# Selective scan with a feed-forward block: VectorE adds the last operand of each half's sums, and TensorE's x projection, a group sum and dt change places with the output projection

## The chip, the cores and the metric

The kernel runs on one core of a Trainium2 chip. The metric is the time on the device of one execution, in microseconds (us), as the median of several runs. Five engines run their own instruction streams in order and meet at semaphores: TensorE (PE, with its weight loads as PEld), VectorE (DVE), ScalarE (ACT), GpSimd (POOL) and SyncE (SP), which issues nearly all DMAs.

## The reference, cut to what matters

Everything is fp32: 4096 rows of 1024. A state-space block with 2048 channels and 16 states per channel is followed by a feed-forward block with dequantised weights.

```python
proj = layernorm(x) @ in_proj_w                    # x and z, 2048 channels each
xc = silu(conv4(x) + conv_b)                       # 4 taps along the rows
dt_r, B, C = rmsnorm of (xc @ x_proj_w.T)          # 64 + 16 + 16
dt = softplus(dt_r @ dt_proj_w + dt_bias)
h_t = exp(dt_t * A) * h_{t-1} + dt_t * B_t * xc_t  # per channel, 16 states
y_t = sum over the 16 states of h_t * C_t
y = (y + D * xc) * silu(z)
x = x + y @ out_proj_w
x = x + layernorm(x) @ W + bias                    # feed-forward
```

The sum over the 16 states and the gating `(y + D * xc) * silu(z)` are what the change touches.

## The kernel before, in words

The 4096 rows are cut into 16 chunks (`c`) of 256 rows (T = 256), the 2048 channels into 8 pairs (`j`) of two 128-channel tiles. One step is one pair of one chunk; steps are numbered S = 8c + j, 128 in all. The chunks overlap as a pipeline: while step (c, j) runs the scan of chunk c, TensorE also does the x input projection and x_proj for chunk c + 1, the output projection for chunk c - 1 and the feed-forward block for chunk c - 2. Steps 1 to 5 of a chunk are alike (plain steps, below). Step 6 has in addition the first layer norm's statistics on VectorE (`norm1_stats`); step 7 the transposes of those rows, the rms norm and the second norm's statistics (`norm2_stats`); step 0 the transposes of the second norm. Chunk 1 has no feed-forward part yet, chunk 0 no output projection either, and chunk 15 no x part any more.

The scan of one pair is 16 units (`unit`, `scan`, `product`, u = 0 to 15), each of two states of one tile, in one of four PSUM banks `hb`. For unit u, ScalarE writes exp(dt*A) into `hb` (L1061), GpSimd makes dt*x*B for four states at a time into `dbx` (L486), VectorE scans in place (L1342) and multiplies by C into `hc` (L1290). Two units make a group of four states; there are eight groups k of a step, four for each tile (half a of the pair, k = 4a + q). For every group:

- GpSimd adds one half of `hc` to the other into `half[:, k % 4]`, 128x512 (`group_sum` of GpSimd, L494), which leaves two operands of 256 columns;
- TensorE adds both operands to the bank `ys[a]` with the identity as weights (`group_sum` of TensorE, L574, two matmuls of 256 columns). ScalarE has put D*x there before (L1080).

After the fourth group of a half VectorE multiplies `ys[a]` by the gate into `ybuf` (`y_gate`, L1301). Below, the gate of half 0 of step S is called y0; it stands behind the product of unit 9. The gate of half 1, y1 (`late_y`), is done in the next step, behind the product of unit 1.

All orders are written out by hand in the bodies of `step`. TensorE's in a plain step (each name a piece of work): ffn (L689), groups 6 and 7 of the step before, out_proj 0, x_proj (L604), out_proj 1 (all out_proj: L767), group 0, x_in_proj 0 (L594), group 1, x_in_proj 1, group 2, out_proj 2, group 3, dt_proj (L624), out_proj 3, z_in_proj 1 (L614), group 4, z_in_proj 0, group 5. In steps 7 and 0 the transposes (L581) stand between, with x_proj behind the first four.

Waits that matter here: x_proj writes into `ys[1]` and waits for y1; z_in_proj 1 writes into `ys[0]` and waits for y0; dt_proj writes into `ys[1]` too and waits until VectorE has taken x_proj's result (`pair_ss`, L1253); VectorE's `add_ffn` (L1272), which stands behind the product of unit 0, waits for ffn; `add_out` (L1272) waits for out_proj 3; ScalarE's softplus (L991, L992) waits for dt_proj, and GpSimd's dtx (L512, L516) for the softplus. ScalarE's `silus` (L1070, L951) stand behind unit 3 and give `xcn`, for which the transposes of steps 7 and 0 and x_proj wait.

## Time and profile before

| | us |
|---|---|
| median of 3 runs (lowest, highest) | 4699.61 (4698.31, 4702.74) |
| the profiled execution | 4697.21 |
| its span | 4695.4 |
| TensorE busy, matmuls | 4448.9 (95%) |
| VectorE busy | 4160.0 (89%) |
| GpSimd busy | 4039.2 (86%) |
| ScalarE busy | 3542.4 (75%) |

The mean granted clock of TensorE is 0.972 of full speed. On the chain of work that ended last TensorE has 59% and VectorE 20%. Matmuls are pipelined: in the timeline the busy time of a group of matmuls includes a tail of about 0.17 us that lies beside the next one; the chain shows them without it. VectorE's instructions overlap their neighbours by 0.08 to 0.09 us in the same way, so what one takes in the stream is read from the start of one to the start of the next.

### The profile page before, as it was taken

The numbers are of one execution on the slowest core, as the hardware profiler recorded it, in microseconds if no ns is written. First come the engines' busy times: TensorE is split into PE (matmuls) and PEld (weight loads), VectorE is DVE, ScalarE is ACT, GpSimd is POOL, SyncE is SP. The second block draws the span as 40 slices with busy tenths as digits, with TensorE's granted clock in tenths as the row PEclk, the third lists the DMA queues.
The fourth block names the chain that finished last, engine by engine and source line by source line (L and its number), as shares of the span: only waits on it lengthen the run. The fifth ranks groups of instructions, "written<-read, shape, count | busy, mean of one in ns | idle before, by whom it ended". The sixth has DMA issues, their size and how long they took to land.

```text
span 4695.4 us, 80181 instructions
## 1 busy us (share of the span) xinstructions
PE 4448.9 (95%) x26656; PEld 4049.0 (86%) x26656; DVE 4160.0 (89%) x5745; ACT 3542.4 (75%) x8848; POOL 4039.2 (86%) x2942
## 2 busy tenths in 40 slices
PE   7788989999999999999999999999999999999889
PEld 6567879989898998989989898998989889898779
DVE  3898989989899998989989899998989989899981
ACT  3777787877778787777877878787787777778760
POOL 0898989989898998989989898998989899899990
PEclk9889999999999999999999999999999999999999
DMA  7324243353434435343353534334353443434232
GB/s 255 130 79 161 99 159 139 114 186 133 173 129 161 145 138 175 124 178 128 123 188 123 177 137 165 137 128 173 138 180 120 145 165 129 165 127 155 90 115 94
DMA packets 160285, 678.56 MB, mean 145 GB/s; under 512 B 21120, under 2 KB 30080, under 8 KB 110720
## 3 DMA queue, kind: packets, MB, share of 16 engines
q1 hardware_dynamic: 141440, 639.88, 39.0%
q10 hardware_dynamic: 18432, 33.56, 1.9%
q8 instruction: 212, 3.47, 0.3%
q14 instruction: 201, 1.65, 0.1%
HBM read 618.32 MB, written 55.05 MB: 143 GB/s over the span
## 4 chain that ended last, share of the span: by engine, by line
PE 59%; DVE 20%; POOL 7%; issue 6%; ACT 5%; DMA 1%; SPq 0%; DVEq 0%; POOLq 0%; ACTq 0%
PE g L767 13%; PE gx L594 13%; PE ys L574 12%; DVE hb L1342 11%; PE ys L614 9%; PE g L689 4%; POOL dbx L486 4%; DVE hc L1290 4%; DVE gx L1238 2%; POOL half L494 2%; PE ys L604 2%; DVE bst L1218 2%; PE gx L581 2%; ACT hb L1061 1%; PE hb L853 1%
## 5 line engine op out<-in xcount | busy, mean ns | idle before, releaser
L1342 DVE TENSOR_TENSOR_SCAN hb<-hb,dbx 128x512 f32<-128x512 f32 x2048 | 2498.0, 1220 | 108.0 <-ACT hb L1061 84.4
L486 POOL TENSOR_TENSOR dbx<-dtx,bb 128x1024 f32<-128x1024 f32 x1024 | 2421.0, 2364 | 60.1 <-DVE hb L1342 34.9
L1061 ACT ACTIVATE hb<-dt,a_neg 128x256 f32<-128x256 f32 x4096 | 1789.5, 468 | 66.3
L494 POOL TENSOR_TENSOR half<-hc 128x512 f32<-128x512 f32 x1024 | 1303.1, 1273 | 135.4 <-DVE hc L1290 120.4
L1290 DVE TENSOR_TENSOR hc<-hb,cb 128x512 f32<-128x512 f32 x2048 | 1378.9, 673 | 0.0
L574 PE MATMUL ys<-half,ident 128*128 128x256 f32 x4096 | 1073.2, 389 | 133.4 <-POOL half L494 119.2
L574 PEld LDWEIGHTS ys<-half,ident 128*128 128x128 f32 x4096 | 757.2, 194 | 254.3 <-POOL half L494 151.3
L767 PEld LDWEIGHTS g<-wo,ybuf 128*128 128x128 f32 x7680 | 954.0, 198 | 20.2 <-issue 1.3
L767 PE MATMUL g<-wo,ybuf 128*128 128x128 f32 x7680 | 966.7, 281 | 0.6 <-issue 0.6
L614 PE MATMUL ys<-xnT,wz 128*128 128x256 f32 x4096 | 928.8, 380 | 1.6 <-DVE ybuf L1301 1.6
L594 PE MATMUL gx<-xnT,wx 128*128 128x256 f32 x3968 | 904.5, 381 | 4.3 <-DMA wx<-in_win 2.6
L1057 ACT COPY hstate<-hb 128x2 f32<-128x2 f32 x2044 | 319.3, 156 | 757.7 <-DVE hc L1290 754.5
L614 PEld LDWEIGHTS ys<-xnT,wz 128*128 128x128 f32 x4096 | 770.6, 191 | 103.1 <-DVE ybuf L1301 2.8
L594 PEld LDWEIGHTS gx<-xnT,wx 128*128 128x128 f32 x3968 | 756.9, 192 | 108.5 <-DMA wx<-in_win 3.0
L689 PEld LDWEIGHTS g<-wf,x2nT 128*128 128x128 f32 x3552 | 414.1, 192 | 5.7
L689 PE MATMUL g<-wf,x2nT 128*128 128x128 f32 x3552 | 414.5, 275 | 0.0
L1301 DVE TENSOR_TENSOR ybuf<-ys,gate 128x256 f32<-128x256 f32 x256 | 107.0, 418 | 237.8 <-PE ys L574 237.6
L1238 DVE SCALAR_TENSOR_TENSOR gx<-xpre,convw,gx 128x256 f32<-128x256 f32 x744 | 302.0, 482 | 13.8 <-ACT gx L942 13.8
L512 POOL TENSOR_TENSOR dtx<-dt,xcs 128x2 f32<-128x2 f32 x128 | 25.3, 198 | 282.7 <-ACT dt L992 176.8
L604 PE MATMUL ys<-xprojw,xcn 128*128 128x96 f32 x1024 | 152.0, 298 | 26.6 <-ACT xcn L951 23.5
L604 PEld LDWEIGHTS ys<-xprojw,xcn 128*128 128x128 f32 x1024 | 143.2, 215 | 33.9 <-issue 21.5
L1067 ACT ACT_TABLE_LOAD x128 | 164.2, 1283 | 2.3
(105 smaller groups left out, 2766.1 us busy)
## 6 DMA issues: line engine op xcount, KB each, us to landing
wz<-in_win SPq DMA_DIRECT2D x128, 1024.0 KB, 4.8
wx<-in_win SPq DMA_DIRECT2D x124, 1024.0 KB, 4.8
wo<-in_wout SPq DMA_DIRECT2D x123, 1024.0 KB, 4.9
wf<-wf_scratch SPq DMA_DIRECT2D x113, 512.0 KB, 3.2
xc_scratch<-xcn ACTq DMA_DIRECT2D x128, 256.0 KB, 2.1
xcs<-xc_scratch SPq DMA_DIRECT2D x128, 256.0 KB, 5.0
bb<-bc_scratch SPq DMA_DIRECT2D x64, 512.0 KB, 7.5
cb<-bc_scratch SPq DMA_DIRECT2D x64, 512.0 KB, 6.7
```

What stands on the lines that cost most here:

```text
L486: nc.gpsimd.tensor_tensor(dbx[:, k % 2, :].rearrange("p (n t) -> p n t", n=NQ), dtx[:, S % 2, a, :].unsqueeze(1).to_broadcast([P, NQ, T]), ...
L494: nc.gpsimd.tensor_tensor(half[:, k % 4, :], hc[:, k % 2, 0:HALF], hc[:, k % 2, HALF:GW], ALU.add).then_inc(halves, 1)
L574: mm = nc.tensor.matmul(ys[a][:, 0:T], ident[:], half[:, k % 4, i * T:(i + 1) * T], start=False, stop=(q == NQ - 1 and i == 1), skip_group ...
L594: mm = nc.tensor.matmul(pair_bank(q)[:, a * T:(a + 1) * T], pair_weights(q)[:, kk, a * P:(a + 1) * P], xnT[:, chunk % 2, kk, :], start=(kk ...
L604: mm = nc.tensor.matmul(ys[1][:, tt * E:(tt + 1) * E], xcn[:, a * T + tt * P:a * T + (tt + 1) * P], xprojw[:, 2 * (q % PAIRS) + a, :], sta ...
L614: mm = nc.tensor.matmul(ys[0][:, a * T:(a + 1) * T], wz[:, kk, a * P:(a + 1) * P], xnT[:, q // PAIRS % 2, kk, :], start=(kk == 0), stop=(k ...
L689: mm = nc.tensor.matmul(g1[:, tt * P:(tt + 1) * P], x2nT[:, kk, tt * P:(tt + 1) * P], wf[:, kk, :], start=(kk == 0), stop=(kk == KH - 1))
L767: mm = nc.tensor.matmul(g1[:, tt * P:(tt + 1) * P], ybuf[:, (1 - st.parity) * PAIRS + kt // 2, (kt % 2) * T + tt * P:(kt % 2) * T + (tt + ...
L1061: ins = nc.scalar.activation(h[:, m * T:(m + 1) * T], dt[:, j % 2, a, :], ACT.Exp, scale=a_neg[:, ds((2 * j + a) * N + 2 * v + m, 1)])
L1238: nc.vector.scalar_tensor_tensor(bank[:, a * T:(a + 1) * T], xpre[:, a, tap:tap + T], convw[:, ds((2 * jq + a) * KC + tap, 1)], bank[:, a ...
L1290: nc.vector.tensor_tensor(hc[:, k % 2, w * UW:(w + 1) * UW], hb[u % 4][:], cb[:, n:n + 2, :].rearrange("p n t -> p (n t)"), ALU.mult).then ...
L1342: nc.vector.tensor_tensor_scan(h[:], h[:], dbx[:, k % 2, w * UW:(w + 1) * UW], 0.0, ALU.mult, ALU.add).then_inc(scans, 1)
```

## The change

VectorE takes over one operand of the last group of each half (k = 3 and k = 7): TensorE does one matmul there in place of two, and a new function `last_sum` adds the other operand, `half[:, 3, T:2T]`, to `ys[a]` in PSUM. It waits for TensorE's matmul of the group. The gate y0 or y1 comes one scan later than before: `last_sum`, scan, gate, where there was gate, scan. GpSimd's sums for k = 3 and k = 7 now also wait until the gate before has been made. On TensorE, x_proj of steps 1 to 6 (and of the others without transposes) stands behind out_proj 1 in place of ahead of it, and group 3 and dt_proj stand ahead of out_proj 2 in place of behind it.

```diff
             def group_sum(S, k):
                 pool.wait_ge(hcs, after(UNITS * S + 2 * k + 2))
                 pool.wait_ge(sum_mm, after(8 * S + k - 3))
+                if k % NQ == NQ - 1:
+                    pool.wait_ge(y_ready, after(2 * S + k // NQ))
...
                 pe.wait_ge(halves, after(8 * SG + k + 1))
-                for i in range(2):
+                for i in range(1 if q == NQ - 1 else 2):
                     mm = nc.tensor.matmul(ys[a][:, 0:T], ident[:], half[:, k % 4, i * T:(i + 1) * T],
-                                          start=False, stop=(q == NQ - 1 and i == 1), skip_group_check=True)
+                                          start=False, stop=(q == NQ - 1), skip_group_check=True)
...
                     else:
                         out_proj(0)
-                        x_proj()
                     out_proj(1)
                     if not (first and st.ffn or last and st.norm1):
+                        x_proj()
                         group(0)
...
                     group(2)
-                    out_proj(2)
                     group(3)
                     dt_proj()
+                    out_proj(2)
                     out_proj(3)
...
+            def last_sum(SP, a):
+                k = NQ * (a + 1) - 1
+                dve.wait_ge(sum_mm, after(8 * SP + k + 1))
+                dve.wait_ge(halves, after(8 * SP + k + 1))
+                nc.vector.tensor_tensor(ys[a][:, 0:T], ys[a][:, 0:T], half[:, k % 4, T:HALF], ALU.add
+                                        ).then_inc(summed, 1)
+
             def y_gate(SP, a):
...
-                dve.wait_ge(sum_mm, after(8 * SP + NQ * (a + 1)))
+                dve.wait_ge(summed, after(2 * SP + a + 1))
...
                     product(1)
+                    late_sum()
+                    scan(3)
                     late_y()
-                    scan(3)
                     product(2)
...
                     product(9)
+                    last_sum(S, 0)
+                    scan(11)
                     y_gate(S, 0)
-                    scan(11)
                     product(10)
```

`late_sum` is `last_sum` of the step before for half 1. The end of the program has one `last_sum` ahead of its last gate.

TensorE in a plain step before, from groups 6 and 7 of the step before to dt_proj (`ys<-half` the group sums, `g<-wo` out_proj, `ys<-xprojw` x_proj, `gx<-xnT` x_in_proj, `ys<-ssmT` dt_proj):

```order
L574 MATMUL ys<-half,ident 128x256 x4
L767 MATMUL g<-wo,ybuf 128x128 x8
L604 MATMUL ys<-xprojw,xcn 128x96 x4
L767 MATMUL g<-wo,ybuf 128x128 x8
L574 MATMUL ys<-half,ident 128x256 x2
L594 MATMUL gx<-xnT,wx 128x256 x8
L574 MATMUL ys<-half,ident 128x256 x2
L594 MATMUL gx<-xnT,wx 128x256 x8
L574 MATMUL ys<-half,ident 128x256 x2
L767 MATMUL g<-wo,ybuf 128x128 x8
L574 MATMUL ys<-half,ident 128x256 x2
L624 MATMUL ys<-ssmT,dtw 128x256 x2
```

The same place with the change:

```order
L579 MATMUL ys<-half,ident 128x256 x3
L772 MATMUL g<-wo,ybuf 128x128 x16
L609 MATMUL ys<-xprojw,xcn 128x96 x4
L579 MATMUL ys<-half,ident 128x256 x2
L599 MATMUL gx<-xnT,wx 128x256 x8
L579 MATMUL ys<-half,ident 128x256 x2
L599 MATMUL gx<-xnT,wx 128x256 x8
L579 MATMUL ys<-half,ident 128x256 x3
L629 MATMUL ys<-ssmT,dtw 128x256 x2
L772 MATMUL g<-wo,ybuf 128x128 x16
```

Groups 6 and 7 have three matmuls in place of four, and so have groups 2 and 3, which now stand together. x_proj (`ys<-xprojw`) has moved behind the 16 matmuls of out_proj 0 and 1, and the third part of out_proj behind dt_proj, next to the fourth.

VectorE around the gate y1 before (`hb` the scans, `hc` the products):

```order
L1272 TENSOR_TENSOR x<-g,x 128x2x128 [waits f_mm,bias_add]
L1342 SCALAR_TENSOR_TENSOR hb<-hb,dbx 128x512 [waits exps,dbxs]
L1290 TENSOR_TENSOR hc<-hb,cb 128x512 [waits scans]
L1301 TENSOR_TENSOR ybuf<-ys,gate 128x256 [waits o_mm,sz_act,sum_mm]
L1342 SCALAR_TENSOR_TENSOR hb<-hb,dbx 128x512 [waits exps]
L1290 TENSOR_TENSOR hc<-hb,cb 128x512 [waits halves,cb_in1,scans]
```

The same place with the change:

```order
L1277 TENSOR_TENSOR x<-g,x 128x2x128 [waits f_mm,bias_add]
L1355 SCALAR_TENSOR_TENSOR hb<-hb,dbx 128x512 [waits exps,dbxs]
L1295 TENSOR_TENSOR hc<-hb,cb 128x512 [waits scans]
L1304 TENSOR_TENSOR ys<-ys,half 128x256 [waits halves,sum_mm]
L1355 SCALAR_TENSOR_TENSOR hb<-hb,dbx 128x512 [waits exps]
L1314 TENSOR_TENSOR ybuf<-ys,gate 128x256 [waits o_mm,sz_act,summed]
L1295 TENSOR_TENSOR hc<-hb,cb 128x512 [waits halves,cb_in1,scans]
L1355 SCALAR_TENSOR_TENSOR hb<-hb,dbx 128x512 [waits exps,dbxs]
```

`ys<-ys,half` is the new addition. It stands where the gate stood and has taken over the gate's wait for `sum_mm`; the gate follows one scan later.

## Rows read from the trace of the kernel before

**Rows 1.** Busy us per engine, then granted clock, steps 1 to 5.

```profile
2108.00:2300.00 192.00, 192.00 (x1177) 176.92 (x1176) 183.83 (x252) 148.96 (x376) 181.63 (x131) 1.00 0.37 128
```

**Rows 2.** Timeline, gates y0, steps 0, 1, 6, 7, 0: start, us, [idle].

```profile
2103.90 0.42 DVE L1301 TENSOR_TENSOR ybuf<-ys,gate 128x256 f32<-128x256 f32 x1 [4.06 <-PE ys L574]
...
2137.10 0.43 DVE L1301 TENSOR_TENSOR ybuf<-ys,gate 128x256 f32<-128x256 f32 x1 [1.44 <-PE ys L574]
...
2304.34 0.41 DVE L1301 TENSOR_TENSOR ybuf<-ys,gate 128x256 f32<-128x256 f32 x1
...
2340.73 0.42 DVE L1301 TENSOR_TENSOR ybuf<-ys,gate 128x256 f32<-128x256 f32 x1 [3.74 <-PE ys L574]
...
2383.78 0.42 DVE L1301 TENSOR_TENSOR ybuf<-ys,gate 128x256 f32<-128x256 f32 x1 [4.07 <-PE ys L574]
```

**Rows 3.** The chain of waits, plain step: start us, us, what.

```profile
2136.20 0.86 PE ys L574 x4
...
2137.93 1.79 PE g L767 x16
...
2148.35 3.57 PE g L689 x32
```

**Rows 4.** Timeline, VectorE, the same step.

```profile
2134.99 0.67 DVE L1290 TENSOR_TENSOR hc<-hb,cb 128x512 f32<-128x512 f32 x1
...
2152.14 0.41 DVE L1272 TENSOR_TENSOR x<-g,x 128x256 f32<-128x256 f32 x1
...
2154.19 0.41 DVE L1301 TENSOR_TENSOR ybuf<-ys,gate 128x256 f32<-128x256 f32 x1
2154.52 1.22 DVE L1342 TENSOR_TENSOR_SCAN hb<-hb,dbx 128x512 f32<-128x512 f32 x1
...
2156.49 1.23 DVE L1342 TENSOR_TENSOR_SCAN hb<-hb,dbx 128x512 f32<-128x512 f32 x1 [0.17 <-ACT hb L1061]
```

**Rows 5.** Timeline, GpSimd, dtx of step 1, half 3 of step 2.

```profile
2138.93 0.20 POOL L512 TENSOR_TENSOR dtx<-dt,xcs 128x2 f32<-128x2 f32 x1 [1.53 <-ACT dt L992]
...
2165.80 1.27 POOL L494 TENSOR_TENSOR half<-hc 128x512 f32<-128x512 f32 x1
```

**Rows 6.** Timeline, TensorE and VectorE, start of step 7.

```profile
2321.29 0.66 PE L581 MATMUL gx<-ident,xrow 128*128 128x128 f32 x4 [0.89 <-ACT xcn L951]
2321.88 1.13 PE L604 MATMUL ys<-xprojw,xcn 128*128 128x96 f32 x8
2323.18 0.66 PE L581 MATMUL gx<-ident,xrow 128*128 128x128 f32 x4 [0.17 <-ACT xnT L926]
...
2321.42 0.41 DVE L1301 TENSOR_TENSOR ybuf<-ys,gate 128x256 f32<-128x256 f32 x1
```

**Rows 7.** Timeline, TensorE and VectorE, start of step 0.

```profile
2358.83 1.13 PE L574 MATMUL ys<-half,ident 128*128 128x256 f32 x4 [2.42 <-POOL half L494]
2362.55 1.12 PE L581 MATMUL gx<-ident,xrow 128*128 128x128 f32 x4 [2.59 <-ACT xcn L951]
2363.45 1.86 PE L604 MATMUL ys<-xprojw,xcn 128*128 128x96 f32 x8
...
2360.71 0.41 DVE L1301 TENSOR_TENSOR ybuf<-ys,gate 128x256 f32<-128x256 f32 x1
```

**Rows 8.** As rows 1, start of step 7, and of step 0.

```profile
2318.00:2326.00 8.00, 6.46 (x45) 5.24 (x44) 7.35 (x10) 7.85 (x15) 7.16 (x4) 1.00 0.33 115
...
2363.00:2370.00 7.00, 7.00 (x40) 6.75 (x38) 3.89 (x5) 4.86 (x12) 4.50 (x4) 0.64 0.67 245
```

**Rows 9.** Timeline, TensorE and VectorE, a step of chunk 1.

```profile
503.76 1.53 PE L574 MATMUL ys<-half,ident 128*128 128x256 f32 x4 [2.41 <-POOL half L494]
...
488.85 0.42 DVE L1301 TENSOR_TENSOR ybuf<-ys,gate 128x256 f32<-128x256 f32 x1 [2.56 <-PE ys L574]
...
523.18 0.42 DVE L1301 TENSOR_TENSOR ybuf<-ys,gate 128x256 f32<-128x256 f32 x1 [2.57 <-PE ys L574]
```

**Rows 10.** Timeline, VectorE, a gate y0 of chunk 15.

```profile
4363.53 0.42 DVE L1301 TENSOR_TENSOR ybuf<-ys,gate 128x256 f32<-128x256 f32 x1 [0.99 <-PE ys L574]
```

More of the change, by code:

```diff
@@ L212, in build_program @@
         a_exp = sem("a_exp")
-        conv, scans, hcs, y_ready = sem("conv"), sem("scans"), sem("hcs"), sem("y_ready")
+        conv, scans, hcs, y_ready, summed = (sem("conv"), sem("scans"), sem("hcs"), sem("y_ready"),
+                                             sem("summed"))
         xp_add, o_add, f_add = sem("xp_add"), sem("o_add"), sem("f_add")
@@ L1352, in late_product, with late_sum @@
                             times_c(S - 1, UNITS - 1)
+                    def late_sum():
+                        if was.scan and not (first and c == 0):
+                            last_sum(S - 1, 1)
                     def late_y():
@@ L1451, in _ @@
             block_add(NC - 3, PAIRS - 1, g1, f_add)
+            last_sum(LAST - 1, 1)
             y_gate(LAST - 1, 1)
```

## The prediction

> **What bounds the kernel now.** I read the gates y0 in VectorE's timeline first, since one comes in each step. Their distances are 33.20 us from step 0 to step 1 and again in each plain step up to step 5 (four more), 34.44 from step 5 to 6 (y0 of step 5 lies at 2137.10 + 4 x 33.20 = 2269.90), 36.39 from 6 to 7, and 43.05 from 7 to the next chunk's step 0 [rows 2]. Together that is 279.88 us for a chunk, and the chunks 2 to 14 repeat it. In the plain steps TensorE is busy all the time, 192.00 of 192.00 us at full clock, VectorE 183.83 and GpSimd 181.63 [rows 1]; VectorE waits 1.44 us at y0 for the group sum [rows 2] and 0.17 us for an exponential [rows 4]. So a plain step is exactly TensorE's work, 33.20 us, while VectorE's own work is 33.20 - 1.44 - 0.17 = 31.59. VectorE alone sets the step from 5 to 6 (no wait at y0), and TensorE ends last again at the gates of steps 7 and 0, where VectorE waits 3.74 and 4.07 us [rows 2].
>
> **The terms of a plain step.** A group sum of two operands takes TensorE 0.86 us [rows 3], one operand 0.43; two go per step, so TensorE's work becomes 33.20 - 0.86 = 32.34. VectorE gets two additions. No row shows a sum written back to PSUM with a plain add; the nearest rows are the gate, which reads the same bank and takes 0.33 us from its start to the next instruction's (2154.19 to 2154.52), and the block addition, 0.33 (2152.14 to 2152.47) [rows 4]. The bounds are 0.26, what its 256 columns take alone if the scan after it covers the rest (half of the 0.67 of a product of 512 columns, less the 0.08 of overlap), and 0.67, that product whole. I take 0.34, since the gate has the same shape and the same bank, and an intervening scan keeps the gate off the addition's result. VectorE then works 31.59 + 0.68 = 32.27 in a plain step, practically as long as TensorE.
>
> The Trainium skill (VectorE: DVE Perf Modes, the section on the TRN2 errata) gives an instruction with a PSUM source 120 cycles beside one per column, which for 256 columns at 0.96 GHz is an estimate of 0.39 us; by it VectorE's step would be 32.37. The trace disagrees for the gate, with its 0.33 us between starts.
>
> **What keeps the step above both.** Two couplings matter once nobody has slack. First, `add_ffn` waits for ffn. From the end of group 3 (2136.20 + 0.86 = 2137.06, [rows 3]) to the end of ffn (2148.35 + 3.57 = 2151.92) TensorE needs 14.86 us, and `add_ffn` starts at 2152.14 [rows 4], so it had only 0.22 us to spare. Out_proj 2 (1.79, [rows 3]) now lies in that stretch, which makes it 16.65 us; VectorE reaches `add_ffn` 2152.14 - 2137.10 = 15.04, now 15.38 us after it starts the addition for half 0. Group 3 has therefore to end 1.27 us before VectorE wants it, or VectorE waits at `add_ffn` instead of at the gate. What was won by moving group 3 forward is handed on to the next wait. Second, group 3 needs GpSimd's half 3. Call T the moment at which VectorE reaches half 0's addition (2134.99 + 0.67 = 2135.66 in the step shown). Dtx starts at T + 3.27 behind ScalarE's softplus [rows 5]. From there GpSimd's own stream to the end of half 3 (2138.93 to 2165.80 + 1.27 = 2167.07) is 28.1 us, less about 0.5 us of waits inside it for scans, so half 3 is there at T + 30.9 and TensorE's single matmul ends at T + 31.4. Ffn then ends at T + 31.4 + 16.65 = T + 48.05. VectorE goes on from `add_ffn` and reaches the next addition for half 0 after 32.27 - 15.38 = 16.9 us, at T + 64.95. That loop spans two steps, 32.48 each, longer than either engine's own 32.3. I forecast 32.5 for a plain step, 0.7 less than now.
>
> **One chunk.** Step 0 to 1: at the gate of step 0 VectorE waits for group 3, so it reaches `add_ffn` 1.27 us ahead of ffn and waits there: 32.3 + 1.3 = 33.6 (now 33.20). Four steps of 32.5: 130.0 (132.80). Step 5 to 6: VectorE's own work, 34.44 + 0.68, with the wait of 0.17 gone and a little coupling: 35.1 (34.44), a loss.
>
> Step 6 to 7: x_proj here still stands behind the first transposes and waits for y1, and y1 is now later by both additions and a scan. It began at 2321.42, the transposes' instruction before x_proj at 2321.29, x_proj at 2321.88, and the next transposes at 2323.18 [rows 6]. Counted from y0 of step 6 (2304.34), y1 now begins at 17.08 + 0.34 + 0.34 + 1.13 = 18.89 and ends at 19.31, so x_proj starts at 19.4 instead of 17.5 and the transposes behind it at 20.3 instead of 18.84: 1.45 us later. Group 3 is 1.79 earlier in the order and 0.43 shorter. That leaves 36.39 + 1.45 - 2.22 = 35.6 us. But TensorE now idles in two pieces close together: from the end of group 7 (15.45, a step that itself begins 0.85 later because z_in_proj 1 waits for y0) to xcn at 17.2, and from 17.9 to 19.4, 3.3 us in all where the same two places had 0.89 and 0.17 [rows 6]. At the same place in step 0 TensorE idles 2.42 and then 2.59 us [rows 7], and behind it the granted clock is 0.64 over 7 us, so partly 1.2 GHz, while at the start of step 7 it is 1.00 [rows 8]. In chunk 1 a single gap of 2.41 us is followed by a slow matmul group, 1.53 us against 1.13 behind the gap of 2.42 [rows 7, 9]. So I expect a slow stretch in step 7 too, of one half of that in step 0. There x_proj takes 1.86 us where it takes 1.13 in step 7, and the first transposes 1.12 where 0.66 [rows 6, 7]; with the out_proj behind, some 2.6 us are lost. Half of it is 1.3: 36.9 us (36.39).
>
> The Trainium skill (TensorE: Matmul & The Clock Gate, Part 1) says that TensorE's clock is either full or half and follows how busy the engine has been. By that rule the slow stretch of step 7 depends on how the gaps fall, and the sum with none would be 1.3 us per chunk lower.
>
> Step 7 to 0: TensorE ends last, through ScalarE's chain to xcn, which starts from a product that comes 0.34 later. Y1 there is in time: it ended at 2361.1 and will end 1.8 us later, while x_proj began at 2363.45 [rows 7]. So 43.05 + 0.34 - 2.22 = 41.2.
>
> The sum is 33.6 + 130.0 + 35.1 + 36.9 + 41.2 = 276.8, which is 3.1 us less per chunk.
>
> **The whole.** From step 0 of chunk 2 to step 0 of chunk 14 there are 12 such chunks: -37. Chunk 14 has no norm-1 work, its steps 1 to 7 gain 0.7 each, the first and last lose 0.4 and 0.7: -3. Chunk 1 has no ffn, and the gate waits 2.57 us for group 3 in each step, behind TensorE's slow stretch; the step is 523.18 - 488.85 = 34.33 [rows 9]. VectorE's own work is that of a plain step without `add_ffn`, 31.59 - 0.33 = 31.26, now 31.94, and group 3 comes 2.2 us earlier, so I take 32.1: 2.2 gained in each of five steps, and the rest of the chunk as above without ffn: -12. Chunk 0 has neither ffn nor out_proj and is set by VectorE: +2 (0 to +5). In chunk 15 VectorE waits at the gates (0.99, [rows 10]) and hides its additions: -2 (-4 to +2). The tail gets one addition. Together -52 on the profiled 4697.2, so 4645. The median of the runs is 2.4 above the profiled execution: 4647.
>
> What costs nothing: GpSimd's new waits for y_ready (the gate asked for is made some ten units before half 3 or half 7 is due), dt_proj ahead of out_proj 2 (ScalarE is held by its exponentials and table loads, so softplus is not earlier), and x_proj behind out_proj 1 in a plain step (TensorE has other work where it would have waited; `pair_ss` stands three units further on). The DMA issues keep their order; wo has over 10 us from out_proj 3 to its next use.
>
> **The rivals.**
>
> 1. No slow stretch in step 7, or a shorter one in step 0 as its first gap closes (2.42 becomes about 0.9, since TensorE arrives 1.8 us later). For: the gaps of 0.89 and 0.17 left the clock at 1.00 [rows 6, 8]. Against: they add up to over 3 us now. It gives 1.3 to 2.6 us more per chunk: 4647 - 16 to 4647 - 34, so 4613 to 4631. Chance 0.26.
> 2. The couplings eat the plain steps: GpSimd, whose stream with the bias in every second step is nearly as long, and ScalarE add waits that I don't see, and a plain step is 32.85; perhaps two slow stretches in step 7 (another 1.3). That is +1.8 to +3 per chunk: 4647 + 23 to + 38, so 4670 to 4685. Chance 0.18.
> 3. Slower than before: VectorE becomes the bound because the addition into PSUM costs more than the gate. With x us per addition instead of 0.34, a chunk has fifteen or so additions on its chain, so it changes by 15(x - 0.34) - 3.1; it turns at x = 0.55. At 0.67, the upper bound above, it is +1.9 per chunk, some +25 with the gain of chunk 1 halved (-6): about 4721. For it: no add into PSUM is shown. Against: the gate's 0.33. Chance 0.07.
> 4. TensorE's saving turns into nothing because `add_ffn` now waits for what the gate waited for: the plain step stays at 33.2 and only the other gains and losses are left, within 10 us of 4700. TensorE's own load falls by 0.86 of 33.20, which speaks against it. Chance 0.05.
>
> **How the numbers follow.** The forecast, 4632 to 4665, has 0.44. About 0.2% (9 us) is what a measurement of this kernel can tell from no change. The forecast and rivals 1 and 2 are faster by more than that: 0.88, less 0.02 for the end of rival 2 that runs over; so faster 0.86, the same 0.07, slower 0.07. The range reaches to the end of rival 2, 4685, and 8 us below the end of rival 1, to 4605, for chunks 0, 1 and 15 at their better bounds.
>
> **What would show it.** Right: y0 (now the additions) 32.3 to 32.7 us apart in plain steps; the wait of 1.44 at the gate gone, with a wait at `add_ffn` of a few tenths, and 1.3 us in step 0; the addition 0.33 to 0.39 from start to start; steps 5 to 6 longer, near 35.1; x_proj of step 7 waiting for the gate, with a granted clock under 1.00 behind it; chunk 1's steps near 32.1. Wrong: an addition above 0.5 us, a plain step over 32.9, or TensorE idle in plain steps for more than 0.5 us.

## The result: 4699.7 to 4677.4 us, less than half of the gain forecast

The changed kernel takes 4677.44 us (median of 5 runs, 4674.43 to 4679.68) beside 4699.74 us before (5 runs). The ratio is 0.995, with a 95% interval of 0.9936 to 0.9965. The forecast was 4647, so 52.6 us were expected and 22.3 came. The size is off by more than half. The number lies in the stated range only where rival 2 had stretched it (4670 to 4685), and rival 2 did not happen, so that is luck.

### The profile after

The busy line of the page has 512 fewer matmul instructions for TensorE (the profile lists two for each matmul of 256 columns, and 256 of these are gone) and 256 more instructions for VectorE:

```profile
PE 4383.7 (94%) x26144; PEld 3956.8 (85%) x26144; DVE 4239.9 (91%) x6001; ACT 3545.9 (76%) x8848; POOL 4029.4 (86%) x2942
```

The additions for half 0 in VectorE's timeline (start, us, idle before them), in the steps 0, 1, 6, 7 and the next 0; they stand where the gates of [rows 2] stood:

```profile
2087.29 0.43 DVE L1304 TENSOR_TENSOR ys<-ys,half 128x256 f32<-128x256 f32 x1 [1.85 <-PE ys L579]
...
2120.72 0.42 DVE L1304 TENSOR_TENSOR ys<-ys,half 128x256 f32<-128x256 f32 x1
...
2286.22 0.42 DVE L1304 TENSOR_TENSOR ys<-ys,half 128x256 f32<-128x256 f32 x1
...
2323.42 0.43 DVE L1304 TENSOR_TENSOR ys<-ys,half 128x256 f32<-128x256 f32 x1 [1.56 <-PE ys L579]
...
2363.75 0.43 DVE L1304 TENSOR_TENSOR ys<-ys,half 128x256 f32<-128x256 f32 x1 [1.85 <-PE ys L579]
```

The wait of 1.44 us in the plain steps is gone. Around y1 of a plain step:

```profile
2201.63 0.42 DVE L1277 TENSOR_TENSOR x<-g,x 128x256 f32<-128x256 f32 x1 [0.33 <-PE g L694]
2201.97 1.22 DVE L1355 TENSOR_TENSOR_SCAN hb<-hb,dbx 128x512 f32<-128x512 f32 x1
...
2203.69 0.42 DVE L1304 TENSOR_TENSOR ys<-ys,half 128x256 f32<-128x256 f32 x1
2204.02 1.22 DVE L1355 TENSOR_TENSOR_SCAN hb<-hb,dbx 128x512 f32<-128x512 f32 x1
2205.15 0.41 DVE L1314 TENSOR_TENSOR ybuf<-ys,gate 128x256 f32<-128x256 f32 x1
```

`add_ffn` (L1277) now waits 0.33 us for ffn, where it had 0.22 to spare, and the addition takes 0.33 from start to start. In step 0 to 1 the same wait is 1.26 us, where 1.27 were forecast:

```profile
2104.00 0.42 DVE L1277 TENSOR_TENSOR x<-g,x 128x256 f32<-128x256 f32 x1 [1.26 <-PE g L694]
```

The distances of these additions, beside the forecast for each:

| step | before | forecast | after |
|---|---|---|---|
| 0 to 1 | 33.20 | 33.6 | 33.43 |
| 1 to 5, each | 33.20 | 32.5 | 32.50 and 32.63 by turns |
| 5 to 6 | 34.44 | 35.1 | 35.25 |
| 6 to 7 | 36.39 | 36.9 | 37.20 |
| 7 to 0 | 43.05 | 41.2 | 40.33 |
| a chunk | 279.88 | 276.8 | 276.46 |

The column "after" shows chunk 7; chunks 4 to 13 are within 0.2 us of it in every step. So in the chunks 2 to 13 the forecast held in sum. The same marks at the borders of the chunks (starts of the gate or addition of the steps 0, 8, 16, 112, 120, 127, and the span) tell where the rest went:

| stretch | before | after | change | forecast |
|---|---|---|---|---|
| to step 0 of chunk 0 | 150.29 | 152.08 | +1.8 | 0 |
| chunk 0 | 269.91 | 274.21 | +4.3 | +2 |
| chunk 1 | 284.92 | 275.31 | -9.6 | -12 |
| chunks 2 to 13 | 3358.01 | 3321.06 | -37.0 | -37 |
| chunk 14 | 268.14 | 265.94 | -2.2 | -3 |
| chunk 15, first seven steps | 225.86 | 243.62 | **+17.8** | -2 |
| the rest | 138.27 | 140.38 | +2.1 | 0 |

Chunk 15 has lost 17.8 us where 2 were to be gained. That is two thirds of the missing 30.

### Chunk 15 in both traces

TensorE in a step of chunk 15, before (start, us, idle before):

```profile
4385.86 1.13 PE L574 MATMUL ys<-half,ident 128*128 128x256 f32 x4 [1.34 <-POOL half L494]
4389.70 2.07 PE L574 MATMUL ys<-half,ident 128*128 128x256 f32 x4 [2.71 <-POOL half L494]
4391.56 3.62 PE L767 MATMUL g<-wo,ybuf 128*128 128x128 f32 x16
4394.98 1.31 PE L574 MATMUL ys<-half,ident 128*128 128x256 f32 x4
4396.13 1.03 PE L624 MATMUL ys<-ssmT,dtw 65*128 65x256 f32 x4
```

The same place after:

```profile
4383.59 1.39 PE L579 MATMUL ys<-half,ident 128*128 128x256 f32 x4 [2.15 <-POOL half L498]
4387.42 2.07 PE L579 MATMUL ys<-half,ident 128*128 128x256 f32 x4 [2.44 <-POOL half L498]
4390.95 1.22 PE L579 MATMUL ys<-half,ident 128*128 128x256 f32 x2 [1.46 <-POOL half L498]
4391.97 1.91 PE L629 MATMUL ys<-ssmT,dtw 65*128 65x256 f32 x4
```

Chunk 15 has no x input projection, so nothing stands between the groups 0, 1, 2 and 3 on TensorE, and it waits for GpSimd's sum at each. Before, out_proj 2 was done while half 3 was in the making. Now group 3 stands in front of it: TensorE idles a third time (1.46 us), and out_proj 2 and everything behind it come that much later, at a lower clock too (mean granted clock over the seven steps 0.84, before 0.92). Ffn is late, and `add_ffn` pays. VectorE in the same step after:

```profile
4375.81 0.42 DVE L1277 TENSOR_TENSOR x<-g,x 128x256 f32<-128x256 f32 x1 [2.89 <-PE g L694]
```

The waits of the first seven steps of chunk 15 (us in total, times, longest), before and then after:

```profile
PE ys L574 <- POOL half L494: 30.5, 17, 2.7
DVE x L1272 <- PE g L689: 6.2, 5, 1.5
DVE ybuf L1301 <- PE ys L574: 6.0, 8, 1.7
```

```profile
PE ys L579 <- POOL half L498: 42.9, 21, 2.7
DVE x L1277 <- PE g L694: 26.0, 7, 4.9
```

TensorE's waits for GpSimd's sums grew by 12 us, and VectorE's waits for TensorE went from 6.2 + 6.0 to 26.0 us. No wait at the additions is left among the larger ones: it has moved to `add_ffn`.

### The profile page after: what moved, and what is told of

Same layout as the page of the kernel before. It is cut to its first block, busy times and chain, and to the rows that moved or that the text cites. A ratio compares the mean times of both kernels' runs of the same rounds, so it can differ in the third digit from the quotient of the medians.

```text
span 4672.6 us, 79670 instructions
## 1 busy us (share of the span) xinstructions
PE 4383.7 (94%) x26144; PEld 3956.8 (85%) x26144; DVE 4239.9 (91%) x6001; ACT 3545.9 (76%) x8848; POOL 4029.4 (86%) x2942
## 4 chain that ended last, share of the span: by engine, by line
PE 64%; DVE 13%; POOL 10%; issue 7%; ACT 4%; DMA 2%; SPq 0%; POOLq 0%; DVEq 0%; ACTq 0%
PE gx L599 14%; PE g L772 13%; PE ys L619 12%; PE ys L579 11%; POOL dbx L487 6%; PE g L694 6%; DVE hb L1355 6%; DVE hc L1295 3%; POOL half L498 3%; PE ys L609 2%; DVE gx L1243 2%; PE ys L629 2%; PE gx L586 1%; PE hb L858 1%; ACT hb L1066 1%
## 5 line engine op out<-in xcount | busy, mean ns | idle before, releaser
L579 PE MATMUL ys<-half,ident 128*128 128x256 f32 x3584 | 962.1, 394 | 117.8 <-POOL half L498 114.7
L772 PEld LDWEIGHTS g<-wo,ybuf 128*128 128x128 f32 x7680 | 933.7, 199 | 14.8 <-issue 2.7
L772 PE MATMUL g<-wo,ybuf 128*128 128x128 f32 x7680 | 935.5, 281 | 2.0 <-issue 2.0
L579 PEld LDWEIGHTS ys<-half,ident 128*128 128x128 f32 x3584 | 655.5, 194 | 264.4 <-POOL half L498 187.7
L609 PE MATMUL ys<-xprojw,xcn 128*128 128x96 f32 x1024 | 158.9, 307 | 52.7 <-DVE ybuf L1314 30.1
L609 PEld LDWEIGHTS ys<-xprojw,xcn 128*128 128x128 f32 x1024 | 147.3, 221 | 61.4 <-DVE ybuf L1314 37.8
L1277 DVE TENSOR_TENSOR x<-g,x 128x256 f32<-128x256 f32 x240 | 99.4, 414 | 98.9 <-PE g L694 68.2
```

The lines of the kernel that those rows point to most:

```text
L579: mm = nc.tensor.matmul(ys[a][:, 0:T], ident[:], half[:, k % 4, i * T:(i + 1) * T], start=False, stop=(q == NQ - 1), skip_group_check=True)
L609: mm = nc.tensor.matmul(ys[1][:, tt * E:(tt + 1) * E], xcn[:, a * T + tt * P:a * T + (tt + 1) * P], xprojw[:, 2 * (q % PAIRS) + a, :], sta ...
L772: mm = nc.tensor.matmul(g1[:, tt * P:(tt + 1) * P], ybuf[:, (1 - st.parity) * PAIRS + kt // 2, (kt % 2) * T + tt * P:(kt % 2) * T + (tt + ...
```

## The experiments

Two theories for the missing gain stood at the start. A: the place of group 3 costs chunk 15 its time. B: the additions and the later gates cost it. Besides, the couplings in the forecast were argued and not shown, so the later runs test them.

### The old order where there is no x projection

```diff
                     group(2)
-                    group(3)
-                    dt_proj()
-                    out_proj(2)
+                    if st.x_job(last):
+                        group(3)
+                        dt_proj()
+                        out_proj(2)
+                    else:
+                        out_proj(2)
+                        group(3)
+                        dt_proj()
                     out_proj(3)
```

> The changed kernel, with out_proj 2 again ahead of group 3 and dt in the steps that have no x input projection (chunk 15 and the last step of chunk 14). Theory A (in chunk 15 nothing stands between groups 0 to 3 on TensorE, so with out_proj 2 moved behind them TensorE idles for GpSimd's sums and hands out_proj 2 on to ffn, for which add_ffn waits): chunk 15's steps fall from 34.6 back to about 32.3 us and the time from 4677 to about 4659 (4655 to 4663). Theory B (the additions and the later gate cost chunk 15 its time): the steps stay near 34.6 and the time at 4677.

Measured: 4652.3 us, ratio to before 0.990 (0.9885 to 0.9914), 25 us below the changed kernel. The first seven steps of chunk 15 take 225.3 us (31.4 to 33.1 each) instead of 243.6; up to the start of chunk 14 no stretch of the table above differs by more than 0.2 us. The waits of the same stretch:

```profile
DVE x L1282 <- PE g L694: 5.2, 4, 1.5
DVE ys L1309 <- PE ys L579: 3.6, 4, 1.4
```

Theory A holds: the additions are all still there and cost chunk 15 nothing. Of the 20.1 us between the two profiled spans, 18.3 lie in these steps and 2.2 in the rest of the program behind them. That accounts for the miss of chunk 15 and of the last stretch. The medians differ by more, 25.1 us: the changed kernel's profiled execution was the fastest of its five and this one's the slowest of its four. So 4652.3 lies a little below the 4655 to 4663 expected.

### The parts alone

Additions and later gates, TensorE's order as before:

```diff
                     else:
                         out_proj(0)
+                        x_proj()
                     out_proj(1)
                     if not (first and st.ffn or last and st.norm1):
-                        x_proj()
                         group(0)
...
                     group(2)
+                    out_proj(2)
                     group(3)
                     dt_proj()
-                    out_proj(2)
                     out_proj(3)
```

> The additions and the later gates alone, TensorE's order as before the change. If x_proj's wait for y1 is what the order change is for: y1 ends 19.4 us after the addition for half 0 begins, x_proj and the 12.6 us behind it end at 33.8, so plain steps take 33.8 us instead of 33.2, step 6 to 7 about 38, and the time is about 4760 (4735 to 4785). Rival: x_proj's wait is hidden, plain steps 32.4, and the time is about 4670.

Measured: 4795.4 us, ratio 1.0203 (1.0188 to 1.0218). A plain step takes 34.04 us. Step 6 to 7 takes 40.4 and 37.35 by turns, from chunk to chunk (step 7 to 0 behind it 42.3 and 43.3). The waits of the whole run have x_proj (L609) behind the gate (L1314) 103 times:

```profile
PEld ys L609 <- DVE ybuf L1314: 167.8, 103, 2.7
```

So the move of x_proj is what makes the additions possible at all: without it TensorE loses more at x_proj than the two matmuls give. The sum was 35 us too low: some 15 in the plain steps and step 0 to 1 (34.04 against 33.8, five in each of 13 chunks), some 11 in step 6 to 7 (38.9 on average against 38).

Additions and x_proj moved, group 3 and dt in their old places:

```diff
                     group(2)
+                    out_proj(2)
                     group(3)
                     dt_proj()
-                    out_proj(2)
                     out_proj(3)
```

> The additions and x_proj behind out_proj 1, but group 3 and dt where they were before. Theory A: no wait at add_ffn and no loop of 32.5, so plain steps take TensorE's own 32.35 us; but steps 6 to 7 and 7 to 0 are 1.8 us longer each than in the changed kernel (39.0, 42.1); chunk 15 is as before the change. About 4678 (4670 to 4688). Rival (group 3's place is what makes plain steps fast): plain steps stay at 33 or more, time above 4695.

Measured: 4700.7 us, ratio 1.0001 (0.9991 to 1.001). As a time it is on the rival's side. Chunk 15 is well (225.5 us), but plain steps take 32.39 and 33.07 by turns, 32.73 on average, not 32.35, and step 6 to 7 takes 40.4 and 37.35 by turns, where 39.0 was expected for each. VectorE waits at the addition for group 3 in each plain step:

```profile
2207.29 0.43 DVE L1304 TENSOR_TENSOR ys<-ys,half 128x256 f32<-128x256 f32 x1 [0.22 <-PE ys L579]
...
2240.36 0.43 DVE L1304 TENSOR_TENSOR ys<-ys,half 128x256 f32<-128x256 f32 x1 [0.90 <-PE ys L579]
```

The expectation that TensorE's own 32.35 would come out was wrong. Group 3's place is worth 0.17 us in a plain step and, in the steps 6 to 7 and 7 to 0 together, 5.2 us in one chunk and 3.1 in the next (40.4 + 42.3 and 37.35 + 43.3 against 37.2 + 40.3); it costs 1.05 in step 0 to 1 (32.39 against 33.44) and 0.4 in step 5 to 6. What delays TensorE in the longer of the two plain steps the timeline shows: group 4 comes 0.29 us later behind z_in_proj 1 than in the shorter step, right behind ScalarE's D*x for the bank, and groups 6 and 7 take 0.26 us more.

The turns of step 6 to 7 are a matter of the clock. TensorE's gaps in step 7 are the same in both chunks, 1.32 or 1.33 us ahead of the first transposes and 1.39 ahead of x_proj. Behind them, in one chunk and in the next (the granted clock is the number ahead of the DMA share):

```profile
2046.00:2049.00 3.00, 3.00 (x14) 3.00 (x15) 2.33 (x3) 1.25 (x4) 2.38 (x2) 0.50 0.02 5
2327.00:2330.00 3.00, 3.00 (x27) 3.00 (x28) 2.28 (x3) 2.53 (x7) 2.38 (x2) 1.00 0.03 5
```

TensorE's order alone (no additions, two matmuls in each group, gates in their old places and waiting for TensorE as before, no new wait on GpSimd):

```diff
-                for i in range(1 if q == NQ - 1 else 2):
+                for i in range(2):
...
-                    late_sum()
-                    scan(3)
                     late_y()
+                    scan(3)
...
-                    last_sum(S, 0)
-                    scan(11)
                     y_gate(S, 0)
+                    scan(11)
```

> TensorE's new order alone: two matmuls for every group, no additions, gates where they were. Theory A: plain steps stay at TensorE's 33.2 us, steps 6 to 7 and 7 to 0 fall to 34.6 and 41.3, step 0 to 1 grows to about 34.8, chunk 15 loses its 18 us just as in the changed kernel: about 4684 (4676 to 4694). Theory B: chunk 15 loses nothing, since no additions are there: about 4665.

Measured: 4681.4 us, ratio 0.9962 (0.9947 to 0.9977). Plain steps take 33.20, step 6 to 7 34.60, 5 to 6 35.87, and 7 to 0 40.2 to 40.3 in most chunks (41.7 in two of twelve). Step 0 to 1 stays at 33.20, where 34.8 was expected. The first seven steps of chunk 15 take 245.9 us. The waits in chunk 15:

```profile
DVE x L1274 <- PE g L691: 26.9, 7, 4.8
```

Here there is no addition, and chunk 15 loses the same as in the changed kernel (26.9 against 26.0 us of waits at `add_ffn`). Theory B is out from this side too. The order gains about as much by itself as the whole change: what it brings lies in the steps 6 to 7 (36.39 to 34.60) and 7 to 0 (43.05 to 40.3), less 1.4 us lost in step 5 to 6. What the additions and the saved matmuls bring lies in the plain steps (33.20 to 32.56), and they give part of it back in step 6 to 7 (34.60 to 37.20). In a plain step of this run the whole wait of the gate has gone over to `add_ffn` (1.59 us), as rival 4 had it; the change is faster there only by TensorE's saved matmuls.

### What an addition costs in place

```diff
-                nc.vector.tensor_tensor(ys[a][:, 0:T], ys[a][:, 0:T], half[:, k % 4, T:HALF], ALU.add
-                                        ).then_inc(summed, 1)
+                dve.sem_inc(summed, 1)
```

> The changed kernel without VectorE's addition: the waits and all places stay, the last operand of each half's sums is left out of the result. It prices the addition in place. With 0.34 us each: plain steps fall from 32.56 us to TensorE's own 32.35, step 5 to 6 from 35.25 to 34.6, steps 6 to 7 and 7 to 0 by 0.35 to 0.7 each; per chunk about 2.5 us less, 4677 to about 4640 (4630 to 4655). If VectorE is nowhere on the path: 4677.

Measured: 4622.6 us, ratio 0.9836 (0.982 to 0.9853). Plain steps take 32.34 and 32.48, step 5 to 6 35.1, 6 to 7 35.05, 7 to 0 40.24. So all additions together cost 55 us, more than the 37 expected. In the plain steps they cost only 0.15 us of the 0.67 they take, largely since the wait at `add_ffn` is 0.74 and 0.84 us without them and 0.33 and 0.46 with them; the largest part is step 6 to 7 with 2.15 us. TensorE at the start of step 7, in the changed kernel and then here:

```profile
2303.49 0.66 PE L586 MATMUL gx<-ident,xrow 128*128 128x128 f32 x4 [1.33 <-ACT xcn L956]
2305.54 2.00 PE L609 MATMUL ys<-xprojw,xcn 128*128 128x96 f32 x8 [1.39 <-DVE ybuf L1314]
```

```profile
2276.45 0.66 PE L586 MATMUL gx<-ident,xrow 128*128 128x128 f32 x4 [1.33 <-ACT xcn L956]
2278.17 1.13 PE L609 MATMUL ys<-xprojw,xcn 128*128 128x96 f32 x8 [1.06 <-DVE ybuf L1313]
```

The second gap is 0.33 us shorter without the addition, and x_proj takes 1.13 us instead of 2.00. The busy time and granted clock (the number ahead of the DMA share) of the stretch behind, again the changed kernel and then this one:

```profile
2306.00:2309.00 3.00, 3.00 (x16) 3.00 (x16) 1.89 (x3) 1.27 (x4) 2.38 (x2) 0.50 0.03 5
```

```profile
2279.00:2282.00 3.00, 3.00 (x28) 2.99 (x28) 2.45 (x3) 2.19 (x7) 2.07 (x2) 1.00 0.03 5
```

That is the slow stretch forecast for step 7: TensorE at 1.2 GHz in the one, at 2.4 GHz in the other. But the next but one run shows that the length of the gaps does not decide it alone.

### A second addition

```diff
+                nc.vector.tensor_tensor(spare[:], ys[a][:, 0:T], half[:, k % 4, T:HALF], ALU.add)
                 nc.vector.tensor_tensor(ys[a][:, 0:T], ys[a][:, 0:T], half[:, k % 4, T:HALF], ALU.add
                                         ).then_inc(summed, 1)
```

> The changed kernel with a second addition of the same operands ahead of each, into a spare tile: VectorE gets 0.33 us more per half. If VectorE is now on the path all through a chunk: plain steps 33.0 to 33.2 us, step 5 to 6 35.9, about 4.5 to 5 us per chunk, 4677 to about 4740 (4725 to 4755). If TensorE or the GpSimd loop still hides it: plain steps stay at 32.6, time about 4690.

Measured: 4721.1 us, ratio 1.0048 (1.0033 to 1.0063), 44 us above the changed kernel where 63 were expected. Plain steps go from 32.56 to 32.83 and step 6 to 7 from 37.20 to 37.87. From none to one addition costs a plain step 0.15, from one to two 0.27. Of the 0.66 us that the second adds, the wait at `add_ffn` (0.33 and 0.46) takes up more than half. Then it is used up: in most plain steps of this run VectorE has no wait at all, so it is the bound. This also puts the point where rival 3 decides to the test. With 0.66 us per half the kernel is slower than before, as that rival had it; the addition takes 0.33.

### The loop over two steps

```diff
+                        if k == 3:
+                            nc.gpsimd.tensor_tensor(spare[:], biasb[:, 0:T], biasb[:, T:2 * T], ALU.add)
                         group_of_b(S, k, c)
```

> The changed kernel with one more GpSimd addition of 128x256 (about 0.6 us) in each step, between dtx and half 3. If the loop of two steps (dtx, half 3, group 3, ffn, add_ffn, and back to VectorE) sets a plain step, it gets 0.6 us longer, half of that per step: plain steps 32.85 us, and with the other steps about 3 us per chunk: 4677 to about 4715 (4700 to 4730). Rival: plain steps are the sum of small waits and not this loop; GpSimd's slack of about 0.7 us per step hides it: plain steps 32.6, time about 4685.

Measured: 4684.6 us, ratio 0.9967 (0.9954 to 0.998). The added instruction takes 0.73 us (median of 128). Four plain steps take 32.62, 33.17, 32.98 and 32.85, on average 32.91, which is 0.35 more than in the changed kernel; half of 0.73 is 0.37. That is the loop's price, and not the rival's. The links of the loop show it too: TensorE now waits visibly for half 3 at group 3, and the wait at `add_ffn` has grown from 0.33:

```profile
2216.74 0.70 PE L582 MATMUL ys<-half,ident 128*128 128x256 f32 x2 [0.25 <-POOL half L499]
```

```profile
2201.34 0.42 DVE L1280 TENSOR_TENSOR x<-g,x 128x256 f32<-128x256 f32 x1 [0.82 <-PE g L697]
```

In the changed kernel itself the loop costs TensorE little. Its chain of waits runs on TensorE alone through the plain steps, and only the groups that need half 7 and half 3 are stretched:

```profile
2201.52 1.49 PE ys L579 x6
...
2216.11 1.39 PE ys L579 x6
```

Six such matmuls take 1.29 us where nothing is missing (four take 0.86). Over two steps these stretches come to some 0.4 us: TensorE's own 32.34 and 0.2 of waits for GpSimd make 32.56.

The time as a whole came out 30 us below what was expected, on the rival's 4685, and that is luck: step 6 to 7 fell from 37.20 to 35.56 in ten of the twelve chunks 2 to 13. TensorE there:

```profile
2303.93 0.66 PE L589 MATMUL gx<-ident,xrow 128*128 128x128 f32 x4 [1.32 <-ACT xcn L959]
2305.98 1.13 PE L612 MATMUL ys<-xprojw,xcn 128*128 128x96 f32 x8 [1.40 <-DVE ybuf L1317]
```

The gaps, 1.32 and 1.40 us, are those of the changed kernel, and yet x_proj takes 1.13 us and the clock stays at 1.00. In the other two chunks (5 and 11) of the same run, behind gaps of the same lengths, the clock falls a little later (0.54 over three microseconds) and the step takes 37.19. So two gaps of this size can bring a slow stretch or not. Its price is the difference, about 1.6 us in a chunk here and 3.1 in the runs with group 3 in its old place. By the forecast's words it depends on how the gaps fall; what of their place decides I have not isolated.

### Filling the gaps of step 7

Out_proj 0 ahead of x_proj, in step 7 only, on top of the first experiment:

```diff
                         norm2(0)
                         norm1(0)
-                        x_proj()
-                        norm2(1)
-                        norm1(1)
-                        out_proj(0)
+                        if first:
+                            x_proj()
+                            norm2(1)
+                            out_proj(0)
+                        else:
+                            out_proj(0)
+                            x_proj()
+                            norm1(1)
```

> The kernel of the first experiment (old order where there is no x projection), and in step 7 out_proj 0 fills the gap ahead of x_proj. If the two gaps of 1.33 and 1.39 us cause the slow stretch in step 7: the second gap goes, the granted clock stays at 1.00, and step 6 to 7 falls from 37.2 to about 34.2 us (1.4 of gap, 1.6 of slow clock): 4652 to about 4615 (4605 to 4630). If the clock falls for the first gap alone: step 6 to 7 about 35.8, time about 4633.

Measured: 4628.9 us, ratio 0.9851 (0.9836 to 0.9865), in the expected range though 14 above its middle; as a time it is nearer to the other theory's 4633. The clock decides between them: it stays at 1.00 though the first gap of 1.33 us is still there. Step 6 to 7 is 34.95 us, and TensorE has a new small wait, for ScalarE's copy of the first transposes:

```profile
2295.85 0.66 PE L586 MATMUL gx<-ident,xrow 128*128 128x128 f32 x4 [0.68 <-ACT xnT L940]
```

In every second chunk step 7 to 0 is 41.4 us, in the others 40.2.

Out_proj 0 ahead of the first transposes and out_proj 1 behind them:

```diff
-                    if first and st.ffn or last and st.norm1:
+                    if first and st.ffn:
...
+                    elif last and st.norm1:
+                        out_proj(0)
+                        norm1(0)
+                        out_proj(1)
+                        norm1(1)
+                        x_proj()
                         norm1(2)
                         group(0)
...
                         norm1(3)
```

> As the run before, but in step 7 out_proj 0 stands ahead of the first transposes and out_proj 1 behind them, x_proj behind the second transposes: both gaps filled, clock 1.00, step 6 to 7 set by VectorE at about 33.5 us (33.3 to 34.5). About 4609 (4600 to 4622). Rival: ScalarE's copies out of the transposes come later and hold up the exponentials, step 6 to 7 35 us or more, time above 4625.

Measured: 4603.3 us, ratio 0.9795 (0.978 to 0.981), the fastest of all. Step 6 to 7 is 33.85 us, 7 to 0 40.2. TensorE has no gap there up to the x input projection, and the clock is full:

```profile
2274.77 2.02 PE L772 MATMUL g<-wo,ybuf 128*128 128x128 f32 x16
2276.63 0.60 PE L586 MATMUL gx<-ident,xrow 128*128 128x128 f32 x4
2277.06 1.95 PE L772 MATMUL g<-wo,ybuf 128*128 128x128 f32 x16
2278.85 0.60 PE L586 MATMUL gx<-ident,xrow 128*128 128x128 f32 x4
2279.29 1.03 PE L609 MATMUL ys<-xprojw,xcn 128*128 128x96 f32 x8
```

```profile
2276.00:2284.00 8.00, 7.13 (x56) 6.43 (x55) 7.45 (x11) 7.70 (x20) 6.98 (x6) 1.00 0.11 36
```

The same order of step 7 put into the kernel before, with nothing else:

```diff
-                    if first and st.ffn or last and st.norm1:
+                    if first and st.ffn:
...
+                    elif last and st.norm1:
+                        out_proj(0)
+                        norm1(0)
+                        out_proj(1)
+                        norm1(1)
+                        x_proj()
```

> The kernel before the change with nothing but step 7's order of the seventh experiment (out_proj 0 ahead of the first transposes, out_proj 1 and the second transposes ahead of x_proj). There the gaps at this place are 0.89 and 0.17 us at full clock, so step 6 to 7 falls from 36.39 by about 1.0 to 35.4 us: 4699 to about 4686 (4680 to 4694). If the reorder were worth as much here as behind the change (3.3 us per chunk), about 4655.

Measured: 4700.9 us, ratio 1.000 (0.999 to 1.001): nothing. Step 6 to 7 falls only to 35.96, and 7 to 0 grows from 43.05 to 43.46. In that step TensorE falls to the lower clock already at group 7:

```profile
2361.55 2.08 PE L574 MATMUL ys<-half,ident 128*128 128x256 f32 x4 [2.42 <-POOL half L494]
```

In the kernel before, the same group took 1.13 us behind the same gap of 2.42 [rows 7]. The reorder is worth 49 us behind the change (4652.3 to 4603.3) and nothing without it.

The lengths of whole chunks tell more than the single steps here. In the chunks 6 to 13 they are 279.86 to 279.92 us before, in this run and in the run with two additions, though steps of the three differ by up to 2.1 us (7 to 0: 43.05, 43.46, 41.36). They are 276.4 to 276.5 in the changed kernel and in the first experiment, and 272.9 to 273.4 in the run without additions and in the fastest. What this run wins in step 6 to 7, it gives back in step 7 to 0, where the granted clock is 0.57 over ten microseconds (2363 to 2373), before 0.66 (2360 to 2370). Why the chunk lengths of different kernels coincide these runs do not show; but a term of a step is not won for good until the slow stretch behind it has been looked at.

## Why the prediction was right and wrong

**Plain steps, right.** 32.56 us against 32.5. VectorE's addition at 0.34 was right (0.33). The two couplings are there: `add_ffn` waits 0.33 us where it had 0.22 to spare, and an instruction of 0.73 us in GpSimd's part of the loop lengthens a plain step by 0.35, half of itself. The marks of the loop lie where the forecast put them. From an addition for half 0 (T = 2185.85) to the end of half 3 it is 30.9 us (forecast 30.9), and to `add_ffn` at 2234.24 48.4 (forecast 48.05 for the end of ffn):

```profile
2185.85 0.42 DVE L1304 TENSOR_TENSOR ys<-ys,half 128x256 f32<-128x256 f32 x1
```

```profile
2215.47 1.27 POOL L498 TENSOR_TENSOR half<-hc 128x512 f32<-128x512 f32 x1
```

The estimate of 0.39 us from the Trainium skill (VectorE: DVE Perf Modes, the section on the TRN2 errata) is not borne out for this shape: the trace has 0.33 between starts.

**Step 0 to 1, 5 to 6, 6 to 7, right.** 33.43, 35.25 and 37.20 against 33.6, 35.1 and 36.9. Step 5 to 6 is VectorE's own work with a wait of 0.33 us at `add_ffn`, as forecast, but the loss there is not the additions' alone: without them the step still takes 35.10, since `add_ffn` then waits 0.76. In step 7 the gaps are 1.33 and 1.39 us, 2.7 together instead of the 3.3 forecast, the clock behind them is 0.50 for three microseconds, and the stretch costs about 1.6 us, not 1.3. Without it the step takes 35.56 (the run with the GpSimd instruction), where the forecast had 35.6. That the stretch came is in part luck: in that run the same gaps leave it out in ten chunks of twelve. The Trainium skill (TensorE: Matmul & The Clock Gate, Part 1) has the clock either full or half, by how busy the engine has been. The trace agrees as to the two levels, 1.00 and 0.50; what the clock follows, gaps of the same lengths with either outcome do not show.

**Step 7 to 0, right in kind.** 40.33 instead of 41.2. TensorE's first gap closed from 2.42 to 0.96 us, as rival 1 had it, while the second grew from 2.59 to 3.01. TensorE's clock over ten microseconds of the start of step 0, before and after:

```profile
2360.00:2370.00 10.00, 7.45 (x40) 7.21 (x40) 6.73 (x10) 7.82 (x16) 7.42 (x7) 0.66 0.77 263
```

```profile
2343.00:2353.00 10.00, 7.43 (x47) 6.93 (x48) 7.06 (x11) 8.54 (x18) 8.73 (x8) 0.83 0.82 331
```

So the forecast's slow stretch in step 7 and the half of rival 1 that concerns step 0 both came true. That the chunk as a whole came within 0.4 us of the forecast is in part luck: this term was 0.9 too high and the others together 0.5 too low, and the chunk lengths of several kernels here coincide in a way that the forecast had no term for.

**Chunk 15, the step that failed.** The prediction put it: "In chunk 15 VectorE waits at the gates (0.99) and hides its additions: -2 (-4 to +2)." It looked at VectorE alone and took the new order on TensorE for free there. The order had been weighed only in the plain steps, where x_in_proj stands between the groups and half 3 is there in time. In chunk 15 it is not: out_proj 2 was the work that covered the wait for half 3. The term was +17.8, with +2.1 in the last stretch, and putting the old order back in those steps gives 25 us back at once (4677.4 to 4652.3; 20 between the two profiled executions). The order alone, without any addition, loses the same there (245.9 us for the seven steps, 243.6 with the change). With -2 for the chunk and 0 for the tail, as forecast, 22 of the missing 30 us are explained.

**Chunks 0 and 1 and the start, too good.** +4.3 instead of +2, -9.6 instead of -12, +1.8 instead of 0: 6 to 7 us together. In chunk 1 a plain step is 32.01 and 33.19 by turns where 32.1 was forecast for each; in chunk 0 the step from 6 to 7 is 38.5 instead of 33.9. With step 7's order of the fastest run (4603.3) that step is 35.1 and chunk 0 takes 270.0 us, as before the change, so its loss lies in step 7's order on TensorE, where the forecast saw only VectorE. The start differs between the kernels by some us in either direction (148.9 to 153.2 in these runs), so +1.8 there says nothing. I have made no run on chunks 0 and 1 by themselves.

**The rivals.** Rival 2, that the couplings eat the plain steps, did not happen. Rival 3, VectorE as the bound, did not happen at 0.33 us per addition, and did when it was doubled. Rival 4 did not happen in the changed kernel; it describes the plain steps of the order alone, 33.20 us.

## What to carry to other kernels

When an instruction is moved, look at every kind of stage in which the moved line runs, above all those at the ends of a pipeline where parts of the work are missing: the neighbours that cover a wait in the middle may not be there. Here 14 chunks gained 49 us by the change, and the first and the last lost 4 and 18. And a shift of an in-order engine's work that lengthens a gap by a third of a microsecond should be priced with the clock as well; filling such gaps with work that is ready (here two parts of out_proj) was worth twice the whole change. The same filling was worth nothing in the kernel before, so such a gain has to be measured in the kernel that it is meant for.

## What the runs showed of the hardware

- Two TensorE gaps of 1.33 and 1.39 us with a transpose group between them were followed by about three microseconds at half clock in the changed kernel, while gaps of 1.32 and 1.40 us at the same place, in the run with the GpSimd instruction added, left the clock at 1.00 in ten chunks of twelve. With group 3 in its old place the same two gaps were followed by 0.50 in one chunk and by 1.00 in the next, all through the run, at a price of 3.1 us. The length of the gaps alone does not tell what the clock does.
- VectorE's add of a PSUM and an SBUF operand of 256 columns takes 0.33 us from start to start into PSUM, the same as into SBUF.
- GpSimd's addition of 128x256 takes 0.73 us, more than half of the 1.27 of 128x512.
